# Batch-norm variances from the covariance about a 13-batch mean, folded with the output projection, and a new order up to turn one

## The reference, cut to what matters

```python
def _L0_cond_ref(x, cs, ...):            # attention
    ...
    out = jnp.einsum('bhij,bhjd->bhid', mod, v).transpose(0, 2, 1, 3).reshape(Bb, Ss, Ee)
    return out @ Wout.T + bout           # x1

def _L0_ffn_ref(x, w_q, bn_gamma, bn_beta, keys, down_embed, up_embed):   # x is x1
    q = jnp.einsum('bnd,de->bne', x, w_q)                 # 2048 features
    mean = jnp.mean(q, axis=(0, 1)); var = jnp.var(q, axis=(0, 1))        # over all tokens
    q = (q - mean) * jax.lax.rsqrt(var + BN_EPS) * bn_gamma + bn_beta
    sim = jnp.einsum('pbnhd,hkpd->pbnhk', q.reshape(...), keys)           # 32 keys a side, 8 heads
    sx, ix = top_k(sim[0], 8); sy, iy = top_k(sim[1], 8)
    scores, pk = top_k(all 64 sums of sx and sy, 8)
    h = gelu(x @ down_embed[indices].T) * softmax(scores)
    return sum over heads and experts of h * up_embed[indices]
```

## Time and profile before

| | us |
|---|---|
| median of 3 runs | 823.06 (821.5 to 825.45) |
| the profiled execution | 821.65 |
| its span | 819.9 |

### The profile page before, as it was taken

The page is one execution under the profiler, slowest core; times in us unless marked ns, Lnnn a source line. Parts: engine busy times, 40 slices in busy tenths (PEclk is TensorE's granted clock), DMA queues, the critical chain, the costliest instruction groups (busy, mean ns, idle before and its releaser), DMA issues.

```text
span 819.9 us, 14537 instructions
## 1 busy us (share of the span) xinstructions
PE 776.7 (95%) x5194; PEld 688.5 (84%) x5194; DVE 547.2 (67%) x1450; ACT 580.6 (71%) x990; POOL 316.5 (39%) x231
## 2 busy tenths in 40 slices
PE   4999999987965999999999999999999999999998
PEld 2888888774964889989998999898999999899987
DVE  3576676347526987797697788679778875843522
ACT  2677676504977977897897788789689888652353
POOL 2122222017957717535461663545257271000000
PEclk9999999997995999999999999999999999999999
DMA  9920000000000000000000000000000000000000
GB/s 309 342 80 2 1 2 1 1 1 1 1 1 0 1 2 1 8 1 2 1 8 1 1 8 1 1 8 1 1 1 8 1 2 8 1 1 1 8 1 7
DMA packets 11015, 16.92 MB, mean 21 GB/s; under 512 B 664, under 2 KB 6976, under 8 KB 10688
## 3 DMA queue, kind: packets, MB, share of 16 engines
q1 hardware_dynamic: 10944, 15.99, 6.1%
HBM read 14.94 MB, written 1.05 MB: 20 GB/s over the span
## 4 chain that ended last, share of the span: by engine, by line
PE 85%; POOL 8%; issue 3%; DVE 3%; DMA 1%; ACT 0%; DVEq 0%; SPq 0%; ACTq 0%; POOLq 0%
PE banks L441 78%; POOL region L390 7%; PE banks L480 4%; PE banks L639 2%; DMA region<-in_pC 1%; DVE HF L1319 0%; PE banks L496 0%; PE banks L671 0%; DVE W_both L1313 0%; DVE W_both L1144 0%; PE banks L730 0%; DVE acc L1454 0%; PE banks L652 0%; POOL x_all L398 0%; DVE cw L1398 0%
## 5 line engine op out<-in xcount | busy, mean ns | idle before, releaser
L390 POOL TENSOR_TENSOR region<-sim 128x1024 f32<-128x1024 f32 x128 | 260.7, 2064 | 101.5 <-DVE top_keys L1270 63.6
L1002 ACT ACTIVATE HF<-banks,lpack 128x256 f32<-128x256 f32 x256 | 105.6, 481 | 55.4 <-PE banks L441 54.5
L937 ACT ACTIVATE region<-region,neg_thr 128x1024 f32<-128x1024 f32 x128 | 143.7, 1153 | 0.2 <-POOL region L390 0.2
L1313 DVE SCALAR_TENSOR_TENSOR W_both<-region,rz_rel,W_both 128x1024 f32<-128x1024 f32 x98 | 136.7, 1395 | 1.5
L441 PE MATMUL banks<-HF,w_sb 128*128 128x256 f32 x512 | 123.0, 384 | 8.6 <-DVE HF L1319 8.6
L441 PEld LDWEIGHTS banks<-f_sb,HF 128*128 128x128 f32 x1024 | 123.7, 192 | 3.4
L943 ACT ACTIVATE region<-region,dtop 128x1024 f32<-128x1024 f32 x114 | 125.6, 1145 | 0.6
L441 PE MATMUL banks<-f_sb,HF 128*128 128x128 f32 x1024 | 124.5, 275 | 0.0
L441 PE MATMUL banks<-cT,f_sb 128*128 128x256 f32 x512 | 122.7, 382 | 0.1
L441 PEld LDWEIGHTS banks<-HF,w_sb 128*128 128x128 f32 x512 | 94.6, 193 | 20.0 <-DVE HF L1319 9.0
L441 PEld LDWEIGHTS banks<-cT,f_sb 128*128 128x128 f32 x512 | 92.1, 190 | 16.3 <-issue 2.9
(11 more groups left out here) (157 smaller groups left out, 1035.6 us busy)
## 6 DMA issues: line engine op xcount, KB each, us to landing
w_sb<-in_w SPq DMA_DIRECT2D x1, 2048.0 KB, 12.7
f_sb<-in_f SPq DMA_DIRECT2D x1, 2048.0 KB, 16.5
region<-in_wq SPq DMA_DIRECT2D x1, 1024.0 KB, 8.9
region<-in_wqT SPq DMA_DIRECT2D x1, 1024.0 KB, 11.1
w_sb<-in_w SPq DMA_DIRECT2D x1, 1024.0 KB, 8.4
out_x<-acc_f SPq DMA_DIRECT2D x16, 64.0 KB, 1.6
region<-in_pA SPq DMA_DIRECT2D x1, 860.5 KB, 4.7
x1T_all<-in_xT SPq DMA_DIRECT2D x1, 768.0 KB, 8.0
```

What stands on the lines that cost most here:

```text
L390: pool.tensor_tensor(S[a][h].rearrange("p (i j) -> p i j", i=NK), sim[a][:, h, :].unsqueeze(2).broadcast_to([P, NK, NK]), sim[a][:, PH + h ...
L937: act.activation(S[a][h], S[a][h], ACT.Prelu, bias=neg_thr[t % 4][:, h:h + 1], alpha=STEEP).then_inc(h_L, 1)
L1002: m = act.activation(HF[e % 2][:, f, :], bank(2 + b, 256 * (f % 2), 256 * (f % 2) + 256), ACT.Gelu_apprx_tanh, bias=L("bf", 4 * e + f, 4 * ...
L1313: v.scalar_tensor_tensor(W[a], S[a][h], rz_rel[a][:, h:h + 1], W[a], ALU.mult, ALU.add).then_inc(h_w, 1)
```

## The change

It does these things:

- **Covariance about a shift.** The mean of the first 13 batches (`SEEN`) is taken during batch 14 (`shift`, `shift_row`). All tiles are centred about it, 12 of them in batch 14, four behind that, two of those straight from `o_s`. The covariance products run in batch 15 and right after it. The difference to the true mean is made good by `delta`, the mean of tiles 13 to 15 less the shift, whose outer product is subtracted by a product of depth 1.
- **To the residual side.** `U`, `out_query` and the wo columns of the load are gone. C is multiplied by Wo on both sides (`cov_w`, `cov_x1`), and `cov_W(c)` multiplies Wq with that.
- **Products summed by VectorE.** Each 128 x 128 piece is multiplied by `wqT_sb` and summed in one `scalar_tensor_tensor` with `accum_out`, 16 in all (`variances(c)`); `T`, its column-sum products and their banks are gone. gamma is multiplied into the keys ahead of time (`kg`), and beta's keys and `wgr` are done in batch 2.
- **First key product with its bias.** For tile 0 the bias is accumulated in bank 6 (`ones` times `kb`, and `x1_first` in place of x1), so `sim_bias` is not awaited; ScalarE copies it.
- **First tiles.** Expert inputs 0 and 1 go through `HF`, that of tile 2 is made early in banks 4 and 5. Head 0 uses the identity in place of a diagonal; the diagonals are made in pieces in other buffers. ScalarE does the steep half of the next head before the exponential of this one.
- **Turn one** has its own tables, VectorE runs its slots in the order 4, 5, 0, 6, 1, 7, 2, 8, 3, 9, ..., GpSimd takes the root before tile 3's pair scores, and the key product of tile 4 moves from slot 0 to 5. Later turns are as before.

The diff, cut to its core (blank lines are left out):

```diff
+SEEN = 13
+NORM_PE = ["shift_row", "cov", "delta", "cov_w", "delta_w", "cov_x1", "CW0", "CW1", "CW2", "CW3", "weff0", "weff1",
            "sim_bias"]
-NORM_DVE = ["mean_col", "mean_bc", "centred0", "centred1", "centred2", "centred3", "x1mean", "x1neg", "kb", "wgr",
-            "cov", "T0", "T1", "vareps0", "T2", "vareps1", "T3", "vareps2", "vareps3",
-            "scale0", "ka0", "scale1", "ka1", "scale2", "ka2", "scale3", "ka3", "weff1", "sim_bias"]
+NORM_DVE = ["kb", "kg", "wgr", "shift_col", "shift_bc", "centred0", "centred1", "centred2", "centred14", "centred3",
+            "centred15", "cov", "cov_w", "cov_x1", "x1mean", "x1neg", "sum0", "var0", "sum1", "var1", "ka0", "sum2",
+            "var2", "ka1", "sum3", "var3", "ka2", "ka3", "weff1"]
+NORM_ACT = ["delta", "delta_row", "minus_delta_row", "weff0", "sim_bias"]
...
+            pool.tensor_tensor(x1_first, cols(x1T_all, 0), x1neg, ALU.add).then_inc(pool_norm, 1)
...
+                def root():
+                    pool.wait_ge(g_msq, g)
+                    pool.tensor_tensor(rms[:, :], msq[:, :], mhalf[:, 0:2], ALU.pow).then_inc(g_rms, 1)
+                if g == 1:
+                    root()
...
+            def shift_row():
+                wait_norm("shift_bc")
+                pe.wait_ge(s_tanh, B)
+                mm(bank(7, 0, P), mean_bc, A("ident")).then_inc(pe_norm, 1)
...
+            def delta_sum(t):
+                m = mm(bank(4, 0, 1), cols(o_all, t), ones[:, 0:1], start=(t == SEEN), stop=(t == B - 1))
...
+            for t in range(7, B - 1):
+                covariance(t)
+            for t in range(SEEN, B - 1):
+                delta_sum(t)
             out_T(B - 1)
+            covariance(B - 1)
+            delta_sum(B - 1)
+            first_inputs(0, 2)
+            wait_norm("cov")
+            mm(bank(3, 0, P), cov, A("woT")).then_inc(pe_norm, 1)
             out_proj(B - 1)
...
+            pe.wait_ge(act_norm, NORM_ACT.index("delta") + 1)
+            mm(banks[0:1, 4, P:2 * P], delta, A("woT")).then_inc(pe_norm, 1)
+            wait_norm("cov_w")
+            mm(bank(5, 0, P), A("woT"), cov_w, start=True, stop=False)
+            first_inputs(2, 3)
+            pe.wait_ge(act_norm, NORM_ACT.index("minus_delta_row") + 1)
+            mm(bank(5, 0, P), delta_rows[0:1, 0:P], delta_rows[0:1, P:2 * P], start=False, stop=True).then_inc(pe_norm, 1)
+            first_inputs(3, 6)
+            def cov_W(c):
                 for k in range(4):
+                    m = mm(bank(2 + c, P * k, P * k + P), wq_sb[:, P * (4 * c + k):P * (4 * c + k) + P], cov_x1)
...
+            wait_norm("cov_x1")
+            for c in range(4):
+                cov_W(c)
+            mm(bank(7), ones, kb, start=True, stop=False)
+            pe.wait_ge(ld_wqT, 16)
+            folded_keys(0)
+            folded_keys(1)
+            first_inputs(6, 8)
+            folded_keys(2)
             pe.wait_ge(s_x1, B)
+            mm(bank(6), ones, kb, start=True, stop=False)
+            folded_keys(3)
+            pe.wait_ge(act_norm, NORM_ACT.index("weff0") + 1)
             wait_norm("weff1")
+            pe.wait_ge(pool_norm, 1)
+            mm(bank(6), x1_first, weff[:, :], start=False, stop=True).then_inc(t_simp, 1)
             mm(bank(7), x1neg, weff[:, :], start=False, stop=True).then_inc(pe_norm, 1)
...
                 for c in range(8):
                     m = mm(bank(2 + 2 * t + c // 4, P * (c % 4), P * (c % 4) + P), S[t][h][:, P * c:P * c + P],
-                           dg[t][:, h, :], start=False, stop=(h == 7 and c % 4 == 3))
+                           dg[t][h] if h > 0 else ident[:, :], start=(h == 0 and c % 4 == 0), stop=(h == 7 and c % 4 == 3))
...
+            expert_inputs(2, 0, 0)
+            expert_inputs(2, 0, 1)
             key_scores(1, 1)
             key_scores(2, 0)
             for h in range(8):
             for h in range(2):
                 weighted(1, h)
             peer_out(0, 0)
-            for h in range(2, 4):
-                weighted(1, h)
+            weighted(1, 2)
             x2_T(0, 0)
-            for h in range(4, 8):
+            for h in range(3, 6):
                 weighted(1, h)
             key_scores(3, 1)
-            expert_inputs(2, 0, 0)
-            expert_inputs(2, 0, 1)
+            for h in range(6, 8):
+                weighted(1, h)
             peer_out(1, 1)
...
+            steep_pairs(0, 0, 0)
+            for n in range(18):
+                if n < 17:
+                    steep_pairs((n + 1) // 8, (n + 1) // 8 % 2, (n + 1) % 8)
+                exp_pairs(n // 8, n // 8 % 2, n % 8)
+                if n == 4:
+                if n == 13:
+                    x2_T(0, 0, 0)
+                    squares(0, 0)
+                if n == 15:
...
+            def scaled_keys_of_weights():
+                for dst, factor in ((kb, "beta"), (kg, "gamma")):
+                    v.tensor_tensor(k3(dst), k3(A("keysT")), A(factor).unsqueeze(2).broadcast_to([P, 16, NK]),
+                                    ALU.mult).then_inc(dve_norm, 1)
...
+            def shift():
+                v.wait_ge(s_oT, SEEN)
+                v.tensor_reduce(small[:, 16:17], o_sum[:, 0:SEEN], AX_X, ALU.add).then_inc(dve_norm, 1)
+                norm_done("shift_col")
+                v.tensor_scalar(mean_bc, ones, small[:, 16:17], 1.0 / (SEEN * P), ALU.mult, ALU.mult).then_inc(dve_norm, 1)
...
+            def centre(c):
+                n = 4 if c < 3 else 2
+                v.wait_ge(pe_norm, NORM_PE.index("shift_row") + 1)
+                v.wait_ge(s_ostore, 4 * c + n)
+                some = o_all[:, 512 * c:512 * c + P * n].rearrange("p (t n) -> p t n", t=n)
+                v.tensor_tensor(some, some, bank(7, 0, P).unsqueeze(1).broadcast_to([P, n, P]),
+                                ALU.subtract).then_inc(dve_norm, 1)
+            def centre_last(t):
+                v.wait_ge(s_os, t + 1)
+                v.tensor_tensor(cols(o_all, t), o_s, bank(7, 0, P), ALU.subtract).then_inc(dve_norm, 1)
...
+                if b == B - 2:
+                    shift()
+                if b == B - 1:
+                    centre_last(B - 2)
+                    centre(3)
                 if more:
                     shifted_scores(b + 1)
+                if b == 2:
+                    scaled_keys_of_weights()
+                if b == B - 2:
+                    for c in range(3):
+                        centre(c)
...
+            for name, n, dst, factor in (("cov", 2, cov, 1.0 / TOK), ("cov_w", 3, cov_w, 1.0), ("cov_x1", 5, cov_x1, 1.0)):
+                v.wait_ge(pe_norm, NORM_PE.index(name) + 1)
+                v.tensor_scalar(dst, bank(n, 0, P), factor, None, ALU.mult).then_inc(dve_norm, 1)
+            def variances(c):
+                v.wait_ge(pe_norm, NORM_PE.index(f"CW{c}") + 1)
+                for k in range(4 * c, 4 * c + 4):
+                    m = v.scalar_tensor_tensor(junk[:, P * k:P * k + P], bank(2 + c, P * (k % 4), P * (k % 4) + P), 1.0,
+                                               wqT_sb[:, P * k:P * k + P], ALU.mult, ALU.mult, accum_out=small[:, k:k + 1])
+                m.then_inc(dve_norm, 1)
+                norm_done(f"sum{c}")
+                v.tensor_scalar(small[:, 4 * c:4 * c + 4], small[:, 4 * c:4 * c + 4], 1e-5, None, ALU.add).then_inc(dve_norm, 1)
+            def scaled_keys(c):
+                v.wait_ge(pool_norm, 2 + c)
+                v.tensor_tensor(k3(ka[:, P * c:P * c + P]), k3(kg[:, P * c:P * c + P]),
+                                rstd[:, 4 * c:4 * c + 4].unsqueeze(2).broadcast_to([P, 4, NK]), ALU.mult).then_inc(dve_norm, 1)
...
+            diagonals(0, 1, 4)
             pair_sums()
             top_pairs(1)
             thresholds(1, 1)
+            diagonals(0, 4, 8)
             key_sums(2, 0)
             top_keys_of(2, 0)
             top_sums(1, 1)
-            diagonals(1)
+            diagonals(1, 1, 8)
             pair_sums()
             top_pairs(0)
             thresholds(2, 0)
             weigh(0, 0)
             add_peer(0, 0)
-            top_sums(2, 0)
             key_sums(3, 1)
             top_keys_of(3, 1)
             pair_sums()
             thresholds(3, 1)
             weigh(1, 1)
             add_peer(1, 1)
+            top_sums(2, 0)
...
+                slots = list(range(16)) if g != 1 else [4, 5, 0, 6, 1, 7, 2, 8, 3, 9, 10, 11, 12, 13, 14, 15]
+                for s in slots:
```

More of the change, by code:

```diff
@@ L409, in turn @@
                         pair_scores(t + 1, 1, h)
[L410 to L414 removed]
+                if new and g > 1:
+                    keep_x2(t - 1, 1)
+                    root()
                 if not peer:
@@ L529, in attend @@
                     project(b + 2)
+                if b == B - 2:
+                    shift_row()
+                if b == B - 1:
+                    for t in range(3, 7):
+                        covariance(t)
                 pe.wait_ge(s_v, b + 1)
@@ L783, in turn @@
                         outputs2(G2, s + 3)
```

(26 more changed lines are left out.)

264 lines of the change are left out of this document (111 added, 153 removed).

## The result

The changed kernel takes 799.2 us (median of four runs, 798.9 to 800.4) where the kernel before, beside it, takes 824.2: a ratio of 0.970, interval 0.967 to 0.973. The forecast was 805.0 with a range of 798.5 to 813.0. The profiled execution took 798.92, its span is 797.1 against 819.9 before, so the trace has to account for 22.8 us.

What follows compares the result with a forecast made beforehand. The prediction took three stages ahead of the TensorE-bound full turns as what could shrink: 8.45 + 8.15 + 1.4 = 18.0 us off 821.65 gives 803.65, and 1.41 for the median gives 805.0 us, range 798.5 to 813.0.

Steps and rivals of the forecast that it cites:

- stage A: From the last product of attention to GpSimd's first pair scores, 30.99 us before; forecast to gain 8.45.
- the row of 24 heads: Sign in GpSimd's pair scores: 24 heads in one row, with no hole before x2 of tile 0.
- the 2.08 a head: Sign on ScalarE: bias and exponential take 2.08 us a head in the new order, 2.22 before.
- the first scores: Sign: GpSimd's first pair scores start at 179 to 182 us, point forecast 180.3; before at 188.75.
- x2 of tile 1: Sign: the residual of tile 1 comes near 234 us, +53.4 from the first pair score; before 250.30.
- the transposes: Sign: transposes of the experts' sum in turn one come near 281 us; before at 299.01.
- Stage B: From GpSimd's first pair scores to the residual of tile 1, 61.55 us before; forecast to gain 8.15.
- Stage C: From tile 1's residual to the transposes of turn one's experts' sum: 47.3 against 48.71, gain 1.4; wrong under 43 or over 52.
- the walk along VectorE: VectorE's work after tile 1's residual added in order: 9.0 + 27.3 + 5 + 6 = +47.3 us.
- short operations each wait out a GpSimd operation: Rival for turn one: five VectorE operations taken as free cost 7 us, giving 812; 22% together with the accumulator.
- Turn one shrinks to TensorE's work: Rival: VectorE's waits for GpSimd go, the stretch after tile 1's residual is 41, 6.3 less, 798.7 us; 12%.
- The clock rival: Rival: TensorE at half clock for all sixteen heads before tile 1's residual, 29 us more, 834; 3%.

Runs made afterwards that it cites:

- the twin: The changed kernel with an unused plain copy of each of the 16 accumulating products put ahead of it: 808.8 us, 0.983 of the kernel before.
- the filled kernel: The twin plus six unused 128-column products on TensorE in its waits between the folded keys: 803.2 us, 0.977 of the kernel before.

## Why the forecast was right, and what in it was not

The time fell into the range, at its lower end, and most mechanisms of the forecast are in the trace; one is not, for VectorE is not the file of stage A. The sizes were off in all three stages, by 4.4, 4.6 and 4.2 us, with signs that cancelled in part. That is luck: with C as forecast, the time would have been 795, below the range. The other 1.1 us of the miss is that the median lay 0.3 above the profiled execution, not 1.41. Of the signs that the prediction named, the row of 24 heads, the 2.08 a head, the turns and the clock (one head at half) came true; the first scores (179 to 182, measured 175.9), the product (0.37, 0.21), x2 of tile 1 (234, 224.7) and the transposes (281, 276.2) did not, and C at 51.5 is just inside its limit of 52.

*Stage A, 12.85 for 8.45.* Attention ended 0.3 later where 0.7 was charged; traces differ by more than that. The term that was mis-sized is the accumulating product, 0.37 taken, 0.21 measured. The lower bound, 0.26 from the nearest plain product, was no bound: a plain one in this place takes 0.20. A group took 1.05 in place of 1.75, the last scaled keys were done at 171.2 in place of 174.4, and TensorE became the file, with which the folded keys ended 3.4 early. The last 1.0 is the clock of the key product: half was weighed in, full it was, with one wait of 0.56 us before it and none in the 9.4 us ahead of that. The prediction's two ends, 179.3 and 181.0, lie 1.7 apart though it names only 0.85 for the clock; from the end of the folded keys to the first scores the changed kernel took 2.70 and the twin, at half clock, 4.47. The Trainium skill (VectorE: DVE Perf Modes, Two Vector instructions with no wait between them) says that an operation which writes its accumulator is two instructions; the trace has the second, 0.08 long, and the next product starts at its start, so that it adds nothing. The 1.3 us later that it would have made at ScalarE's price did not come.

*Stage B, 12.76 for 8.15.* The order of events is that of the forecast. ScalarE started at +6.0 and needed 2.08 a head; the heads ended at +43.7 in place of +45.1. VectorE's chain for tile 3 started 1.1 earlier (+40.2 for +41.3) and took 4.9 in place of 6.6, all of the difference in the pair sums (0.69 for 2.40), and peer_out took 2.05 in place of 3.78. The last two were on the lower bound that the prediction named (+49.8), and past it: +48.8. The experiments show how near the other value was: in four of the eleven kernels with this stage the pair sums were long, by a start 0.07 to 0.4 us later, and with them peer_out took 3.50 to 3.78, at the half clock or nearly so. Where they were short, with the same work up to that point, peer_out took 2.05 three times, and 2.82, 2.92, 3.12, 3.17 and 3.21. So part of this gain is not a property of the code.

*Stage C, 2.76 lost for 1.4 won.* Here the step that failed is the walk along VectorE. From +9.5 it is full, as forecast, and takes 42.0 us where the walk had 38.3. Three weight sums were priced at 5 us together; the eleven in the full part take 19.9 us, where the eight of before in the same part took 11.8, so the three cost 8. Seven of the eleven took 1.27 to 1.30 each, as a weight sum alone does; three took 2.73, 2.97 and 3.01 beside GpSimd's heads, where none of those eight took over 1.84, and the mean of the eleven of the whole stage rose from 1.62 to 1.77 us. The gate's products went the same way (prob 1.48 for 0.70). The prediction had this as a rival ("short operations each wait out a GpSimd operation", +7 us) and gave it a chance with the accumulator; about half of that size happened, mostly in long operations. The claim that hidden1 ahead of the keys is "no gain by itself" was wrong, at least beside ScalarE's new list: without it C is 5.9 longer and the next tile 2.1 later still. It had looked at VectorE's sum of work; ScalarE's new list, which "ends close behind VectorE at worst" in the text, does so only with VectorE's new one.

*The rivals.* "Turn one shrinks to TensorE's work" gave the nearest time, 798.7, for a reason that did not happen (C at 41). The clock rival (834) did not happen: of the sixteen heads in stage B the first alone ran at half (3.78 for sixteen records at 185.18, at a granted clock of 0.50; 2.02 at 202.05). But the clock was more of a danger than the text had it, at another place: in stage A, where the forecast priced it at 1.7 us between its two ends, the twin shows 4.3.

*Open:* no run isolates the move to the residual side, the first key product with its bias, or the diagonals of stage B, so how the gains of A and B divide among them is not shown. Why attention ends up to 1.3 us earlier in some traces of the same code, and what decides peer_out's clock in stage B, were not tried. Whether ScalarE's old order of turn one (ten first halves ahead) with VectorE's new one would beat both was not tried.

## What to carry to other kernels

Price an unknown operation from its neighbours on both sides, and let the lower end go below the nearest row: the range then holds what the point misses. Before you call the order of one engine's list worth nothing, walk the lists of the other engines in the same stage, for the cover that one order needs may be what another took away. When two kernels share a stage and one of them is a tenth of a microsecond later at an operation that competes for a port, allow for a whole operation of the other engine, and after it for the half clock.

## What the runs showed of the hardware

- An accumulating product of VectorE, 128 by 128 with one operand in PSUM: 0.28 long, its accumulator read 0.08, the next one 0.21 after it. A plain one between two of them takes no less (0.20 to 0.21). Plain ones in turn one of the kernel before: 0.26.
- In the twin TensorE waited 0.59, 0.89 and 0.42 us between its folded keys, and from 172.95 to 183.0 its granted clock was 0.50 (1.2 GHz). In the filled kernel the waits left were 0.20 each and the clock stayed at 1.00 (2.4 GHz): six unused products gained 4.3 us of stage A.
- VectorE's 512-element sum beside GpSimd's heads: 0.69 when it started at +3.65 to +3.67 behind the start of GpSimd's run, 2.2 to 2.5 when it started at +3.74 or later (eleven kernels).
